# Binary 3x3 convolution: the sign images with one zero between rows, so that a tile's input under a tap is one unbroken run

## The reference, cut to what matters

```
x: (64, 256, 28, 28) f32;  M: (256, 256, 3, 3);  Z: (8, 256, 256, 3, 3);  alpha: (256, 1, 1);  rv: (1, 8)

A   = M * M + sum_k Z[k] * Z[k] / 100
bw  = sign((rv @ Z)[0] * rsqrt(A) + M * rsqrt(A))          # weights of -1 and 1
g   = group_norm(x, groups=32, eps=1e-5)
ba  = sign(g)                                              # inputs of -1, 0 and 1
out = x + alpha * conv3x3(ba, bw, padding=1)
```

## Time and profile before

| | |
|---|---|
| median of 3 runs | 542.02 us (541.94 to 542.55) |
| profiled execution, own time | 543.91 us |
| its span, first to last instruction | 542.2 us, granted clock 0.981 |
| TensorE matmuls, busy | 502.3 us (93%), 2794 records |
| TensorE weight loads, busy | 404.7 us (75%) |
| VectorE busy | 371.9 us (69%) |
| ScalarE busy | 328.6 us (61%) |
| GpSimd busy | 23.0 us (4%) |
| DMA | 124.37 MB, 229 GB/s mean |

### The profile page before, as it was taken

The page is one execution under the profiler, slowest core; times in us unless marked ns, Lnnn a source line. Parts: engine busy times, 40 slices in busy tenths (PEclk is TensorE's granted clock), DMA queues, the critical chain, the costliest instruction groups (busy, mean ns, idle before and its releaser), DMA issues.

```text
span 542.2 us, 8289 instructions
## 1 busy us (share of the span) xinstructions
PE 502.3 (93%) x2794; PEld 404.7 (75%) x2794; DVE 371.9 (69%) x711; ACT 328.6 (61%) x566; POOL 23.0 (4%) x70
## 2 busy tenths in 40 slices
PE   0897959899999999999999999999999999999991
PEld 0443538688888888888888888888888888888881
DVE  1122457657967967977868868769778778776646
ACT  1776766477567567666676676676666666754310
POOL 8200000000000000000000000000000000000000
PEclk9998997989999999999999999999999999999997
DMA  7999947018658558568468468468467577434226
GB/s 236 395 393 393 384 173 315 0 70 287 228 188 297 212 201 299 191 222 301 177 214 299 174 216 297 181 220 301 173 236 284 183 248 271 182 141 178 81 98 237
DMA packets 45644, 124.37 MB, mean 229 GB/s; under 512 B 3632, under 2 KB 3632, under 8 KB 45616
## 3 DMA queue, kind: packets, MB, share of 16 engines
q1 hardware_dynamic: 45616, 124.01, 63.2%
HBM read 72.62 MB, written 51.38 MB: 229 GB/s over the span
## 4 chain that ended last, share of the span: by engine, by line
PE 85%; SPq 4%; DMA 4%; DVE 3%; ACT 2%; issue 2%; DVEq 0%; ACTq 0%
PE conv_ps L339 81%; SPq L230 4%; DMA m_sb<-in_L_conv_M_dram 4%; PE conv_ps L279 1%; DVE x_sb L683 1%; PE conv_ps L292 1%; ACT whole L395 1%; DVE bn L608 1%; PE grp_ps L322 1%; PE conv_ps L282 1%; PE conv_ps L296 0%; ACT signs L444 0%; DVE whole L658 0%; PE wt_ps L312 0%; DVE low L590 0%
## 5 line engine op out<-in xcount | busy, mean ns | idle before, releaser
L339 PE MATMUL conv_ps<-signs,wts 128*128 128x448 f32 (+2 forms) x1926 | 444.7, 393 | 2.4 <-ACT signs L444 2.0
L339 PEld LDWEIGHTS conv_ps<-signs,wts 128*128 128x128 f32 x1926 | 366.4, 191 | 72.8 <-ACT signs L444 2.5
L452 ACT ACTIVATE part<-conv_ps 128x448 int32<-128x448 f32 (+2 forms) x107 | 60.0, 561 | 166.3 <-PE conv_ps L339 166.3
L658 DVE SCALAR_TENSOR_TENSOR whole<-conv_ps,part 128x448 int32<-128x448 f32 (+2 forms) x107 | 69.1, 646 | 94.7 <-PE conv_ps L339 84.1
L444 ACT ACTIVATE signs<-x_sb,shift,rstd 128x784 fp32r<-128x784 f32 x128 | 126.0, 1037 | 0.8 <-DVE shift L645 0.8
L666 DVE SCALAR_TENSOR_TENSOR low<-whole,conv_ps 128x448 f32<-128x448 int16 (+2 forms) x107 | 68.8, 643 | 3.7
L683 DVE SCALAR_TENSOR_TENSOR x_sb<-whole,alpha_sb,x_sb 128x784 f32<-128x784 int16 x64 | 65.9, 1030 | 0.7
L683 DVE SCALAR_TENSOR_TENSOR x_sb<-low,alpha_sb,x_sb 128x784 f32<-128x784 f32 x64 | 65.8, 1028 | 0.0
L627 DVE BATCH_NORM_STATS2 bn<-x_sb 128x6 f32<-128x392 f32 x116 | 59.7, 556 | 1.0 <-issue 0.7
L425 ACT ACTIVATE unread<-x_sb 128x784 bf16<-128x784 f32 x58 | 49.1, 847 | 0.0
L423 ACT ACTIVATE unread<-x_sb 128x784 bf16<-128x784 f32 x58 | 49.1, 847 | 0.0
(11 more groups left out here) (46 smaller groups left out, 149.1 us busy)
## 6 DMA issues: line engine op xcount, KB each, us to landing
x_sb<-in_x_dram SPq DMA_DIRECT2D x64, 784.0 KB, 5.7
out_dram<-x_sb SPq DMA_DIRECT2D x64, 784.0 KB, 3.9
x_sb<-in_L_conv_Z_dram SPq DMA_DIRECT2D x64, 288.0 KB, 8.0
m_sb<-in_L_conv_M_dram SPq DMA_DIRECT2D x8, 288.0 KB, 9.7
alpha_sb<-in_L_conv_alpha_dram SPq DMA_DIRECT2D x2, 0.5 KB, 2.4
rv_sb<-in_L_conv_rv_dram SPq DMA_DIRECT2D x1, 4.0 KB, 2.4
```

The lines of the kernel that those rows point to most:

```text
L339: mm = pe.matmul(conv_ps[bank(b)][:, 0:columns(b)], wts[:, ch, tap], e, start=n == 0, stop=n == PRODUCTS - 1, skip_group_check=True)
L452: nc.scalar.activation(part[:, bank(b), 0:columns(b)], conv_ps[bank(b)][:, 0:columns(b)], ACT.Copy, scale=-FRACTION / PACK, bias=FRACTION ...
L658: nc.vector.scalar_tensor_tensor(out=image_tile(whole[:, t % 2], b), in0=flat_tile(conv_ps[bank(b)][:, 0:columns(b)], b), scalar=FRACTION ...
```

## The change

A sign image has rows of 29 values (`PITCH` = W + 1): 28 signs and one zero. That zero is the right border of its row and the left border of the next. An image thus takes 30 x 29 + 2 = 872 values. The output is computed with the same pitch: a tile is a run of consecutive columns over the pitch-29 image, in which every 29th column is of no use and is skipped later. The input of a tile under a tap is then one run, shifted by kh x 29 + kw. The tops have 17 rows (17 x 29 - 1 = 492 columns); the rest of an image, 318 columns, is split into 160 and 158, so the side tiles have 3 x 160 = 480 and 3 x 158 = 474 columns, each with one run per image. The single image has 492 and 318. `whole` and `low` keep the pitch of 29 (812 values per image), and `outputs` reads rows of 28 out of 29 from them. The number of instructions, their order, the semaphores and the DMAs stay.

```diff
-TOP = 16
+TOP_ROWS = 17
...
-    SIDE = (H - TOP) // 2
+    PITCH = W + 1
+    SPAN = H * PITCH
     TILES = TRI + 2
-    TOP_PIX = TOP * W
-    SIDE_PIX = SIDE * W
+    TOP_PIX = TOP_ROWS * PITCH - 1
+    MIDDLE = TOP_ROWS * PITCH
+    REST = SPAN - 1 - MIDDLE
+    SIDE_PIX = (REST // 2 + 1, REST // 2 - 1)
...
-    PH, PW = H + 2, W + 2
+    SIGNS = (H + 2) * PITCH + 2
...
-        signs = sb("signs", [P, 2 * TRI, HALVES, PH * PW], F32R)
+        signs = sb("signs", [P, 2 * TRI, HALVES, SIGNS], F32R)
...
-        whole = sb("whole", [P, 2, TRI, PIX], I32)
-        low = sb("low", [P, 2, TRI, PIX], F32)
+        whole = sb("whole", [P, 2, TRI, SPAN], I32)
+        low = sb("low", [P, 2, TRI, SPAN], F32)
...
-            return TOP_PIX if b < TRI else TRI * SIDE_PIX if b < TILES else 2 * SIDE_PIX
+            return TOP_PIX if b < TRI else TRI * SIDE_PIX[b - TRI] if b < TILES else REST
...
             if b == TILES:
-                return v[:, 0, TOP_PIX:PIX]
-            return v[:, :, TOP_PIX + (b - TRI) * SIDE_PIX:TOP_PIX + (b - TRI + 1) * SIDE_PIX]
+                return v[:, 0, MIDDLE:MIDDLE + REST]
+            start = MIDDLE + (0, SIDE_PIX[0])[b - TRI]
+            return v[:, :, start:start + SIDE_PIX[b - TRI]]
...
-                    v = signs[:, t % 2 * TRI:(t % 2 + 1) * TRI, ch].rearrange("p j (a b) -> p j a b", b=PW)
-                    if b < TRI:
-                        e = v[:, b, kh:kh + TOP, kw:kw + W]
-                    elif b == TILES:
-                        e = v[:, 0, TOP + kh:H + kh, kw:kw + W]
-                    else:
-                        row = TOP + (b - TRI) * SIDE + kh
-                        e = v[:, :, row:row + SIDE, kw:kw + W]
+                    shift_by = kh * PITCH + kw
+                    e = image_tile(signs[:, t % 2 * TRI:(t % 2 + 1) * TRI, ch, shift_by:shift_by + SPAN - 1], b)
...
-                    o = signs[:, t % 2 * TRI + j, h].rearrange("p (a b) -> p a b", b=PW)[:, 1:H + 1, 1:W + 1]
+                    o = signs[:, t % 2 * TRI + j, h, PITCH:(H + 1) * PITCH].rearrange(
+                        "p (a b) -> p a b", b=PITCH)[:, :, 1:W + 1]
...
-                    o = x_sb[:, slot_of(t, j), h]
+                    v = v.rearrange("p (a b) -> p a b", b=PITCH)[:, :, 0:W]
+                    o = x_sb[:, slot_of(t, j), h].rearrange("p (a b) -> p a b", b=W)
```

## The result

The changed kernel takes 533.09 us (median of 4 runs, 532.87 to 533.95), the one before 542.28 us beside it; the ratio is 0.983, with an interval from 0.981 to 0.985. That is 9.2 us faster. The forecast was 35 us faster, 507 us, with a range that ended at 515.

What follows compares the result with a forecast made beforehand. TensorE's matmul stream was taken as the bound, slowed by breaks in its input. Terms of -35.7 - 0.6 + 0.6 + 0.15 + 0.5 = -35.0 us from 542.02 gave 507 us, range 497 to 515.

Steps and rivals of the forecast that it cites:

- What bounds the kernel: Convolution matmuls: TensorE's stream sets the pace, 20.66 us a triple; VectorE (16.4 us after) and ScalarE (13.7) stay hidden.
- I take the excess as 2.5 ns per matmul and 1.7 ns per run: Convolution matmuls at full clock: time above one column per cycle priced by runs; fewer runs gain 1.70 us a triple.
- The row of unbroken float32: Weight stage: 288 unbroken values took 242.5 ns, 2.5 above two cycles each; read as evidence that breaks cost the time.
- Alignment isn't the cause: Convolution input: taps start at even and odd values, yet 18 matmuls of one tile lie between 373 and 384 ns.
- Rival A: TensorE's input: pace set by values, 0.482 ns per column whatever the pattern; 557 us, slower; chance 0.10.
- Rival B: TensorE's input: half of the excess stays, from a cause of each kind; 19.9 us a triple, 531 us; chance 0.06.
- Rival C: Outputs: VectorE becomes the bound because rows of 28 are dear to it; some 583 us were their time doubled; chance 0.02.
- The small terms: Losses outside the full-clock triples: +0.6 us in half-clock stretches, +0.15 in the wait for signs, +0.5 in the tail.
- Half clock: Two convolution stretches at granted clock 0.50: 410 ns for 492 columns against 373, costing +0.6 us.
- Tail: End of the kernel, VectorE working without a break: TensorE's savings on its last 22 matmuls have no effect, +0.5 us.
- The wait for signs: TensorE's 2.02 us wait before the second half-clock stretch: gets 0.15 us longer.

Runs made afterwards that it cites:

- experiment 9: Changed kernel, top tiles of three in four triples reading short runs on a 16-byte line or two values off: 384 columns took 176 or 342 ns.
- experiment 2: Changed kernel, tap starts lowered to multiples of 2, 4 or 128 values in three of four triples: 492 columns stayed at 221 to 225 ns.
- experiments 5: Changed kernel, top tiles of three in four triples reading 16 rows of 28 at gaps 0 to 22: 203.7 ns at gap 0, 228.6 at gap 8.
- experiment 6: Changed kernel without its shared zero, rows of 30 values and every tile one unbroken run: 547.8 us, 1.008 of the kernel before.
- experiment 11: Kernel before with the shared zero alone (pitch 29, old tiles), beside the changed kernel on one chip: 529.89 us against 532.72 us.

## Why the prediction was wrong, step by step

**What bounds the kernel: right.** TensorE's stream sets the pace before and after, and the others stay hidden as forecast (16.40 and 13.69 us).

**"I take the excess as 2.5 ns per matmul and 1.7 ns per run": this step failed.** The step before it had said rightly that the input's arrival is the limit at 2.4 GHz and not at 1.2, and that the three shapes can't part breaks from columns. A third quantity ran along with both: how many lines of 16 bytes a tile touches. n successive values at any start touch n / 4 + 0.75 lines on average. For 448, 504 and 336 columns at pitch 30 the rows cover stretches of 478, 3 x 178 and 358 values, that is 120.25, 135.75 and 90.25 lines; 4.5 + 1.765 each gives 217, 244 and 164 ns, against 215.8, 242.9 and 162.9. The changed tiles touch 123.75, 122.25 and 120.75 lines: 223, 220 and 218, against 224, 222 and 218. Over a product of five tiles that is 632.25 lines before and 614.25 after. The gain is 18 lines x 18 products x 1.765 ns = 0.57 us a triple by this rule, 0.42 measured; the 0.15 between them is some 1.7 ns a matmul, the rule's error over the nine shapes of experiment 9 being up to 5. With a gap of two values a break costs about what fetching two values costs, 2 x 0.44 = 0.9 ns, half of the 1.7 forecast; the rest of the old excess belongs to the values themselves and stays, 18 ns on 492 unbroken columns where the forecast left 4.

**The row of unbroken float32** was read as evidence for the breaks, with the doubt noted that it ran at half the pace per value. That doubt was the point: two cycles a value at 2.4 GHz ask for a line each 3.3 ns in a strip, and in the convolution lines come each 1.8 ns. A stream that asks for half as much can't show the limit of one stream.

**"Alignment isn't the cause"** was true of an unbroken run (experiment 2) and of pitch 30, where a gap of two values leaves hardly any line out, so the count is the same whatever the start. It isn't true in general (experiments 5 and 9). The row could hardly have shown more: it gives durations, which overlap, and not distances, and only at pitch 30.

**Rival A** had the right kind of cause, a pace set by the values that are fetched, but it priced each column at 0.482 ns, with the skipped values booked on the columns. At pitch 30 the skipped ones were fetched already; the change takes 2502 values to 2430, where A has 2352 columns growing to 2430. **Rival B** (half the excess stays, 531 us) came nearest in time, by luck: it put half of the cause on the breaks, and experiment 6 shows that removing them at the old pitch brings nothing. In the trace 492 columns are 18 ns above their 205 where 448 were 29 above their 187. **Rival C** didn't come: outputs unchanged at 1.03 us.

**The small terms.** Half clock: 410 ns for 492 columns, as forecast; but the +0.6 us assumed stretches as long as before, and the first held seven distances at half clock instead of eleven, the second seven as before. In the runs of one chip beside each other (experiment 11) the first held eleven or twelve and there was no second, so this term can't be read from one trace. Tail: 11.2 us, as forecast. The wait for signs before 105.43 us, 2.02 us before, is 2.08 by the timeline, where 2.17 was forecast. The Trainium skill's distance of columns / 2.4 + 2.5 ns (TensorE: Matmul & The Clock Gate, Back-to-back issue gap) is met by the unbroken 2-byte input (207.5 by the rule, 208 measured for 492 columns) and not by the 4-byte one (224). The Trainium skill's 16-byte lines (Advanced Engine Details and Errata, Memory Cachelines) are what the runs show: with 4-byte values the steps fall at multiples of 4. That section speaks of full performance while accesses hit the same line; an unbroken float32r stream was still 6% short of it here.

**Not settled.** Why single taps lie up to 12 ns from the line count (gap 22, and rows one value behind a line), and why the first distance after a block of short matmuls is longer. Whether the pace of lines belongs to the memory or to TensorE's reading of one stream wasn't tried. One row speaks against a limit on all reads together: in the weight stage a round of four records, one a strip, takes 242.5 ns and reads 4 x 72 lines if each record reads its own input, 0.84 ns a line. The rows don't show whether it does.

## What to carry to other kernels

For float32r input at full clock, count the 16-byte lines that each matmul touches, at 1.8 ns each, beside the columns at 0.42 ns; whichever is more sets the distance. This holds to some 5 ns for a tile over all its taps. Gaps of one or two values cost about what they cover, lines wholly inside a gap nothing, and a short run that starts off a line can cost one line more. Making the input unbroken is no aim in itself, and here it wasn't worth the added columns: the shared zero with the old tiles was 2.8 us faster than with the unbroken ones. When several quantities grow together in the shapes of a trace (columns, runs, values covered), a row that is to decide between them must itself run at the pace in question.

## What the runs showed of the hardware

- Unbroken float32r input sustains 0.44 ns a value at granted clock 1.00 (256 to 500 columns, plus 4 to 6 ns), bfloat16 input the array's 0.417 ns (492 columns in 208 ns). At granted clock 0.50 float32r input keeps up exactly (492 columns in 410 ns).
- 384 columns took 176 ns in runs of four on a line and 342 ns in the same runs two values off; in runs of two, one to a line, they took 340.
- Weight loads of 128, 64 or 32 float32 columns made no difference beside 492 columns (their records last 188, 134 and 108 ns). With 128 weight columns the distance stayed at 100 to 110 ns for 64 to 192 input columns; whether the load sets that floor wasn't tried.
- VectorE read rows of 28 out of 29 values (4 and 2 bytes) at the same 1.03 us as 784 in a row.
